# Latent attention: the key tiles' exponentials added on VectorE before one sum over partitions on TensorE

## The chip, the cores and the metric

The kernel runs on one core of one Trainium2 chip, in one launch. The metric is the device time of that core in microseconds (us). Five engines work in parallel, each in its own order: TensorE (PE, matmuls, with its weight loads PEld), VectorE (DVE), ScalarE (ACT), GpSimd (POOL) and SyncE (SP, DMA issues). They wait for one another through semaphores. SBUF is the on-chip memory, PSUM the memory into which PE writes.

## What is computed

The reference runs eight sub-layers one behind another (four attention or state-space layers, four feed-forward ones) over 16 sequences of 512 tokens with 128 features. The change is in the third, a causal attention with 16 heads whose keys and values come from a latent of 32 features:

```
q_blhd = jnp.einsum('bld,dhk->blhk', x_bld, Wq)
latent_bll = jnp.einsum('bld,dc->blc', x_bld, Wkv_down)
k_blhd = jnp.einsum('blc,chk->blhk', latent_bll, Wk_up)
v_blhd = jnp.einsum('blc,chk->blhk', latent_bll, Wv_up)
attn = jnp.einsum('bqhd,bkhd->bhqk', q_blhd, k_blhd) / jnp.sqrt(jnp.asarray(HD, dtype=x_bld.dtype))
attn = jax.nn.softmax(jnp.where(mask, attn, neg_inf), axis=-1)
y_blhd = jnp.einsum('bhqk,bkhd->bqhd', attn, v_blhd)
return jnp.einsum('bqhd,hdo->bqo', y_blhd, Wout)
```

The softmax needs, for every query and head, the sum over the keys of the exponentials. That sum is what the change computes in another way.

## The kernel before

The kernel has three loops, over sub-layers 1 to 4, 5 to 8 and the end. Each takes two sequences (`PAIR`) in a pass, so the first loop has eight passes, and each of them holds the latent attention once.

The 16 heads of the two sequences are worked in eight quartets of four heads (`QUARTETS`, c = 0 to 7). The 512 keys of a head lie in four tiles of 128, key tile m with the 512 - 128m queries that may see it: 512, 384, 256 and 128 columns, 1280 a head. A quartet has six steps (u = 0 to 5), two heads in each: steps 0 and 1 handle key tile 0, steps 2 and 3 key tile 1, steps 4 and 5 key tiles 2 and 3 together. In step (c, u) of `twin_attention`

- PE computes the transposed scores of quartet c (keys on partitions, `scores_t`, L1779, with the negated row maxima added by a bf16 matmul, L1790) and the plain scores of quartet c + 2 (queries on partitions, `scores`, L1761). Both go to one of three double PSUM banks, `twin`, handed round in turn: a matmul waits until the bank's last reader is done.
- DVE takes the row maxima of the plain scores (`maxima`, L792), two quartets ahead. A maximum is two instructions, the operation and a read of the accumulator.
- POOL splits a quartet's maxima into three bf16 parts (`split`, L615 to L625), PE turns them (`turn_max`, L1843), ACT copies them (`take_max_rows`, L1463).
- ACT takes the exponentials of the transposed scores into one of six buffers of `at_pt` in `arena` (`exponents`, L1435), and POOL sets the masked corner to zero (`mask`, L597 and L601).
- PE multiplies the exponentials with the latent values (`values`, into bank 6) and with ones (`sums`, into bank 7), both in `weigh` (L1802), in matmuls with 32 output rows, one for each of the four heads.
- ACT turns the sums into reciprocals (`invert`: logarithm L1454, exponential L1456), and DVE multiplies the values with them (`divide`, L806).

For the sums this means 16 matmuls a quartet over all 1280 columns of each head, with b = 0, 1, 2 for the steps' pairs. In the program each fp32 matmul is one instruction; in the trace it is two. The order of an engine's work is the order in which the functions are called at the end of each step; in between the engines wait on counts of semaphores. The last quartets (c = 6, 7) have no plain scores and no maxima beside them, since there is no quartet c + 2; the values and sums of quartet 7 end in a ninth round.

`ring` is an SBUF tensor of six rows of 512 that other layers use.

## Time and profile before

| | us |
|---|---|
| median of 3 runs | 6033.78 |
| lowest, highest | 5996.2, 6043.12 |
| span of the profiled execution | 6032.4 |
| PE busy in it | 4713.6 (78%) |
| DVE busy | 3697.0 (61%) |
| ACT busy | 1851.2 (31%) |
| POOL busy | 2161.3 (36%) |

The profiled execution is one execution of the program. Times inside it are counted from its first instruction. Busy time of an engine is the time covered by its instructions; matmuls overlap one another, so a group of them is priced by the distance between starts. In the timeline each row is a run of like instructions: start, length, engine, line, operation, output and inputs, shapes, and how many there are. A row of windows names its stretch and its length, the busy time (and count of instructions) of PE, PEld, DVE, ACT and POOL, the granted clock, the DMA share and GB/s. A bracket at the end of a timeline row is the idle time in front of it and who ended it. PEclk is the granted clock of PE, 1.00 for 2.4 GHz and 0.50 for 1.2 GHz.

### The profile page before, as it was taken

To read this page: it belongs to the slowest core of one execution; us is meant where nothing else is said; L and a number is where in the kernel's file an instruction comes from. 1 tells how busy PE (TensorE), PEld (TensorE's weight loads), DVE (VectorE), ACT (ScalarE), POOL (GpSimd) and SP (SyncE) were. 2 spreads that over 40 slices of the span, in tenths; PEclk is the share of its full clock that TensorE was granted. 3 is DMA by queue.
4 is the path that set the end of the run, shared out by engine and by line. 5 is a ranking of instruction groups with operands and counts; after the bars stand their busy time and mean duration, and the time that the engine had idled before them with its cause. 6 is when DMAs were issued, how large, how long until landed. Compare 5 with 4: busy or idle time off the path is not lost. (4 is left out here: it accounts for less than half of the span.)

```text
span 6032.4 us, 97232 instructions
## 1 busy us (share of the span) xinstructions
PE 4713.6 (78%) x37160; PEld 2735.5 (45%) x37160; DVE 3697.0 (61%) x11081; ACT 1851.2 (31%) x2829; POOL 2161.3 (36%) x2704
## 2 busy tenths in 40 slices
PE   5979797979797979595877868778687786877772
PEld 3444445444444444363443544535435444354442
DVE  3646464646464646364768567686686766857765
ACT  2333343334333334242323224132331322412320
POOL 1323232323232222444525236153361443614525
PEclk9989898989898989797888888888888888888886
DMA  4000000000000000372000000000000000000000
GB/s 146 6 18 6 18 6 18 6 18 6 18 6 18 6 18 6 112 232 74 4 15 13 8 20 4 15 14 6 18 6 12 18 5 17 8 9 20 3 15 5
DMA packets 141914, 146.71 MB, mean 24 GB/s; under 512 B 31256, under 2 KB 126042, under 8 KB 141042
## 3 DMA queue, kind: packets, MB, share of 16 engines
q1 hardware_dynamic: 114274, 93.48, 5.3%
q0 software_dynamic: 18432, 37.79, 2.2%
q10 hardware_dynamic: 8736, 8.91, 0.5%
q8 instruction: 326, 5.34, 0.4%
q14 instruction: 146, 1.20, 0.1%
HBM read 69.64 MB, written 62.59 MB: 22 GB/s over the span
## 5 line engine op out<-in xcount | busy, mean ns | idle before, releaser
L792 DVE CUSTOM_DVE_ANT_0 twin<-twin,w_mask_row 128x512 f32<-128x512 f32 (+3 forms) x2048 | 951.0, 521 | 329.7 <-PE twin L1761 328.3
L1761 PE MATMUL twin<-arena 32*128 32x128 f32 (+3 forms) x4096 | 799.4, 517 | 39.6 <-DMA arena<-hres 16.8
L1779 PE MATMUL twin<-arena 32*128 32x128 f32 (+3 forms) x4096 | 784.2, 499 | 35.3 <-DVE arena L792 33.9
L1707 PE MATMUL twin<-w_ident_b 128*128 128x512 bf16 x1536 | 454.9, 450 | 383.7 <-DVE mv L752 157.9
L1435 ACT ACTIVATE arena<-twin 128x768 f32<-128x768 f32 (+1 forms) x544 | 479.3, 881 | 691.6 <-PE twin L1790 387.5
L1779 PEld LDWEIGHTS twin<-arena 32*128 32x128 f32 x4096 | 342.8, 195 | 471.7 <-issue 283.3
L695 POOL TENSOR_SCALAR ve<-mv 128x4 f32<-128x4 f32 x128 | 27.7, 216 | 1467.8 <-DVE mv L752 1467.2
L321 POOL DMA_INDIRECT got<-sorted_y,back x288 | 281.1, 976 | 539.6 <-ACT ring L1641 289.0
L1707 PEld LDWEIGHTS twin<-w_ident_b 128*128 128x128 bf16 x1536 | 157.7, 112 | 651.5 <-DVE mv L752 180.6
L313 POOL DMA_INDIRECT sorted_x<-got,w_mo_first_slots x288 | 282.4, 981 | 467.5 <-DVE ring L866 302.2
L1761 PEld LDWEIGHTS twin<-arena 32*128 32x128 f32 x4096 | 353.6, 204 | 196.8 <-issue 109.2
L1802 PE MATMUL twin<-arena 128*32 128x128 f32 (+3 forms) x2944 | 305.8, 459 | 18.6 <-POOL arena L597 18.6
L792 DVE DVE_READ_ACCUMULATOR2_ANT arena<- 128x1 f32 x2048 | 292.4, 143 | 0.0
L597 POOL TENSOR_SCALAR_AFFINE_SELECT arena<-arena 128x256 f32<-128x256 f32 x352 | 143.0, 409 | 342.7 <-ACT arena L1435 342.5
L1435 ACT ACTIVATE ring<-twin 128x768 f32<-128x768 f32 (+1 forms) x224 | 194.0, 878 | 198.6 <-PE twin L1779 197.6
L701 POOL TENSOR_TENSOR rs<-ve,minus_half 128x4 f32<-128x4 f32 x208 | 223.6, 1075 | 17.3
L2180 PE MATMUL twin<-w_l3f_we,arena 128*128 128x128 f32 x1152 | 191.1, 320 | 47.7 <-DVE arena L1115 47.7
L651 POOL TENSOR_TENSOR w_mo_wgu<-w_mo_wgu,w_l_cs_feat 128x2048 f32<-128x2048 f32 x36 | 197.3, 5483 | 54.5 <-DVE w_mo_wgu L1364 27.7
L1802 PE MATMUL twin<-ring,arena 128*32 128x384 f32 (+3 forms) x1152 | 155.7, 497 | 64.1 <-POOL ring L597 57.5
L651 POOL TENSOR_TENSOR w_mo_wgu<-w_mo_wgu 128x2048 f32<-128x2048 f32 x36 | 200.3, 5568 | 13.5 <-DVE w_l_wo L1367 13.5
L2180 PEld LDWEIGHTS twin<-w_l3f_we,arena 128*128 128x128 f32 x1152 | 163.9, 221 | 88.9 <-DVE arena L1115 63.6
L1364 DVE TENSOR_REDUCE w_mo_wgu<-w_mo_wgu 128x128 f32<-128x1024 f32 x144 | 174.6, 1217 | 22.6 <-POOL w_mo_wgu L651 22.6
(440 smaller groups left out, 10008.1 us busy)
## 6 DMA issues: line engine op xcount, KB each, us to landing
sorted_y<-arena SPq DMA_DIRECT2D x96, 256.0 KB, 2.8
sorted_x<-zeros ACTq DMA_DIRECT2D x2, 4096.0 KB, 19.9
a<-sorted_x SPq DMA_DIRECT2D x64, 128.0 KB
b<-sorted_x SPq DMA_DIRECT2D x64, 128.0 KB, 2.5
hres<-sorted_x SPq DMA_DIRECT2D x64, 128.0 KB
sorted_x<-got,w_mo_first_slots POOLq DMA_INDIRECT x288
got<-sorted_y,back POOLq DMA_INDIRECT x288
x_out<-w_l_w SPq DMA_DIRECT2D x18, 256.0 KB, 2.3
```

Of the source, the lines that this page charges most:

```text
L313: pool.indirect_dma_start(sorted_x[r % GROUPS], bass.IndirectOffsetOnAxis(ap=slot_of[:, q, n:n + 1], axis=0), normed[q][:, r // GROUPS], N ...
L321: pool.indirect_dma_start(got[q][:, n], None, sorted_y, bass.IndirectOffsetOnAxis(ap=back[:, q, n:n + 1].bitcast(U32), axis=0)).then_inc(s ...
L651: pool.tensor_tensor(pr, left.broadcast_to(shape), right.broadcast_to(shape), ALU.mult).then_inc(sg["f_pool"], 1)
L701: pool.tensor_tensor(RS[q][:], VE[q][:], minus_half[:], ALU.pow).then_inc(sg["rstd_ready"], 1)
L792: last = dve.tensor_tensor_reduce(s[:, e, at:at + w], s[:, e, at:at + w], W["mask_row"][:, T - w:T], -1.0, 3e38, ALU.add, ALU.min, into)
L1364: i = dve.tensor_reduce(ht_sc[q][:, t, heads], ht_pr[m % 2].rearrange("p (h g d) -> p h g d", h=H, g=H)[:, heads], AX, ALU.add)
L1435: act.activation(at_pt[tag][n % len(at_pt[tag])][:, :, 0:w], twin[SLOT["scores_t", c, u] % 3][:, :, 0:w], ACT.Exp, scale=1.0 if tag == "l1 ...
L1707: pe.matmul(into, ident_b, ident_b.unsqueeze(1).broadcast_to([P, NT, P]), start=True, stop=True, skip_group_check=True)
L1761: last = pe.matmul(s[:, e, at:at + w], queries[r, P * i:P * (i + 1)], keys[r, 0:w], start=(at == 0), stop=True, skip_group_check=True)
L1779: last = pe.matmul(s[:, e, at:at + w], keys[r, P * m:P * (m + 1)], queries[r, P * m:T], start=(at == 0), stop=(tag == "l2"), skip_group_ch ...
L1802: last = pe.matmul(bank[into][rows_of(j), P * m:T], weights(m, j), at_pt[tag][n % len(at_pt[tag])][:, j % 2, at:at + w], start=(m == 0), s ...
L2180: i = pe.matmul(pb3(q, 3)[:, t], mo_fb[q][:, (e - 1) % 2, t * P:(t + 1) * P], weights[:, (e - 1) * P:e * P], start=(e == 1 and t == 0), st ...
```

## The change

DVE adds the exponentials of a head's key tiles where they share queries, into a new tile `at_sum` (two buffers in `ring`, 2 x 2 heads x 384 columns). Queries 0 to 127 see key tile 0 alone; their sum stays a matmul of 128 columns straight from the exponentials (`first_sums`). For queries 128 to 511 DVE adds tile 1 to tile 0 (`merge_first`, 768 elements for two heads), tile 2 to that (`merge_second`, 512) and tile 3 (`merge_third`, 256), and PE sums the result over the partitions once, with 384 columns a head (`merged_sums`). The sums of a quartet are 8 matmuls in place of 16. The exponentials now also wait until the additions and the first sums have read their buffer. `turn_max`, `values(c - 1, 2)`, `divide`, `invert` and `take_max_rows` move by one step. Layer 5's attention, which uses the same functions with the tag "l2", keeps its work and order.

```diff
+        at_sum = [ring[:, 3 * n:3 * (n + 1)].rearrange("p a t -> p (a t)").rearrange("p (h e k) -> p h e k", h=2, e=2)
+                  for n in range(2)]
...
+                            def merge_first(c, h):
+
+                                if not 0 <= c < QUARTETS:
+                                    return
+                                dve.wait_ge(sg["l1_masked"], STEPS_OF * c + 3 + h)
+                                if c >= 2:
+                                    dve.wait_ge(sg["l1_sums"], c - 1)
+                                dve.tensor_tensor(at_sum[c % 2][:, h], at_pt["l1"][h][:, :, P:T], at_pt["l1"][2 + h][:, :, 0:T - P],
+                                                  ALU.add).then_inc(sg["l1_merged"], 1)
+
+                            def merge_second(c, h):
...
+                                into = at_sum[c % 2][:, h, :, P:T - P]
+                                dve.wait_ge(sg["l1_masked"], STEPS_OF * c + 5 + h)
+                                dve.wait_ge(sg["l1_merged"], STEPS_OF * c + 2)
+                                dve.tensor_tensor(into, into, at_pt["l1"][4 + h][:, :, 0:2 * P], ALU.add
+                                                  ).then_inc(sg["l1_merged"], 1)
+
+                            def merge_third(c, h):
...
+                                into = at_sum[c % 2][:, h, :, 2 * P:T - P]
+                                dve.wait_ge(sg["l1_merged"], STEPS_OF * c + 3 + h)
+                                dve.tensor_tensor(into, into, at_pt["l1"][4 + h][:, :, 2 * P:3 * P], ALU.add
+                                                  ).then_inc(sg["l1_merged"], 1)
...
                                     beside(c, u)
-                                    if tag == "l2" and u == 1:
-                                        shift(c + 1)
-                                    if u == (2 if tag == "l1" else 5):
+                                    if tag == "l2":
+                                        if u == 1:
+                                            shift(c + 1)
+                                        elif u == 5:
+                                            divide(c - 1)
+                                    elif u < 2:
+                                        merge_second(c - 1, u)
+                                        if u == 1:
+                                            merge_third(c - 1, 0)
+                                            merge_third(c - 1, 1)
+                                    elif u == 3:
                                         divide(c - 1)
+                                    elif u >= 4:
+                                        merge_first(c, u - 4)
...
+                                    if tag == "l1":
+                                        act.wait_ge(sg["l1_merged"], STEPS_OF * (c - 1) + (1 + u % 2 if u < 4 else 5 + u % 2))
+                                        if u < 2:
+                                            act.wait_ge(sg["l1_first_sums"], c)
...
-                                    if tag == "l1" and u == 1:
+                                    if tag == "l1" and u == 2:
                                         invert(c - 1)
-                                    if tag == "l1" and u == 2:
+                                    if tag == "l1" and u == 3:
                                         take_max_rows(c + 1)
...
+                            def first_sums(c):
...
+                                for j in range(HG):
+                                    last = pe.matmul(bank[7][rows_of(j), 0:P], W["ones"][:, 0:LAT],
+                                                     at_pt["l1"][1 - j // 2][:, j % 2, 0:P], start=True, stop=True,
+                                                     skip_group_check=True)
+                                last.then_inc(sg["l1_first_sums"], 1)
+
+                            def merged_sums(c):
...
+                                pe.wait_ge(sg["l1_merged"], STEPS_OF * (c + 1))
+                                for j in range(HG):
+                                    last = pe.matmul(bank[7][rows_of(j), P:T], W["ones"][:, 0:LAT],
+                                                     at_sum[c % 2][:, 1 - j // 2, j % 2], start=False, stop=True,
+                                                     skip_group_check=True)
+                                last.then_inc(sg["l1_sums"], 1)
...
                                         elif u == 1:
-                                            sums(c - 1, 2)
+                                            values(c - 1, 2)
                                         elif u == 2:
+                                            merged_sums(c - 1)
+                                        elif u == 3:
                                             turn_max(c + 1)
-                                            values(c - 1, 2)
-                                        elif u == 3:
-                                            sums(c, 0)
                                         elif u == 4:
                                             values(c, 0)
                                         else:
-                                            sums(c, 1)
+                                            first_sums(c)
```

On PE, in the latent attention of a pass, the place is steps 0 to 3 of the second quartet (c = 1). `w_ones` marks the sums over partitions, `w_ident_b` the turned maxima, the other rows with 32 partitions the values. Before:

```order
L1802 MATMUL twin<-arena 32x384 x4
L1779 MATMUL twin<-arena 128x512 x2
L1790 MATMUL twin<-arena,w_ones_b 128x512 x2
L1761 MATMUL twin<-arena 128x512 x2
L1802 MATMUL twin<-arena,w_ones 32x256 x4
L1802 MATMUL twin<-arena,w_ones 32x128 x4
L1779 MATMUL twin<-arena 128x384 x2
L1790 MATMUL twin<-arena,w_ones_b 128x384 x2
L1761 MATMUL twin<-arena 128x384 x2
L1843 MATMUL twin<-w_ident_b,arena 128x128 x4
L1802 MATMUL twin<-arena 32x256 x4
L1802 MATMUL twin<-arena 32x128 x4
```

The same place in the changed kernel:

```order
L1847 MATMUL twin<-arena 32x384 x4
L1824 MATMUL twin<-arena 128x512 x2
L1835 MATMUL twin<-arena,w_ones_b 128x512 x2
L1806 MATMUL twin<-arena 128x512 x2
L1847 MATMUL twin<-arena 32x256 x4
L1847 MATMUL twin<-arena 32x128 x4
L1824 MATMUL twin<-arena 128x384 x2
L1835 MATMUL twin<-arena,w_ones_b 128x384 x2
L1806 MATMUL twin<-arena 128x384 x2
L1873 MATMUL twin<-ring,w_ones 32x384 x4
```

The values of key tiles 2 and 3 have moved one step forward, to where the sums of those tiles were, and the one sum of the added tile stands behind the scores of step 2; the turned maxima follow a step later.

On DVE the place is steps 5, 0 and 1 (`L794` are the maxima, each with its readout). In the changed kernel:

```order
L794 ISA twin,arena<-twin,w_mask_row 128x128
L794 ISA arena 128x1
L828 TENSOR_TENSOR ring<-arena 128x768
L794 ISA twin,arena<-twin,w_mask_row 128x512
L794 ISA arena 128x1
L794 ISA twin,arena<-twin,w_mask_row 128x512
L794 ISA arena 128x1
L838 TENSOR_TENSOR ring<-ring,arena 128x2x256
```

and then, behind the maxima of step 1:

```order
L794 ISA arena 128x1
L838 TENSOR_TENSOR ring<-ring,arena 128x2x256
L847 TENSOR_TENSOR ring<-ring,arena 128x2x128 x2
L794 ISA twin,arena<-twin,w_mask_row 128x384
```

Before, nothing stood between the maxima of these steps; the only other work was the divide behind those of step 2.

## Rows read from the trace of the kernel before

**Rows 1.** The page: busy time of each engine; POOL's mask (count, busy us, mean ns).

```profile
PE 4713.6 (78%) x37160; PEld 2735.5 (45%) x37160; DVE 3697.0 (61%) x11081; ACT 1851.2 (31%) x2829; POOL 2161.3 (36%) x2704
...
L597 POOL TENSOR_SCALAR_AFFINE_SELECT arena<-arena 128x256 f32<-128x256 f32 x352 | 143.0, 409 | 342.7 <-ACT arena L1435 342.5
```

**Rows 2.** Windows of one quartet with maxima beside it, and one without.

```profile
270.10:283.10 13.00, 13.00 (x152) 5.99 (x152) 8.51 (x33) 6.82 (x10) 6.02 (x14) 1.00 0.03 11
309.00:322.00 13.00, 13.00 (x123) 5.02 (x124) 1.38 (x2) 7.02 (x10) 5.20 (x9) 1.00 0.05 17
```

**Rows 3.** Timeline of PE in the first pass: start us, us, what.

```profile
266.91 0.86 PE L1802 MATMUL twin<-arena,w_ones 128*32 128x256 f32 x16
267.70 0.59 PE L1779 MATMUL twin<-arena 32*128 32x384 f32 x2
...
268.76 0.40 PE L1843 MATMUL twin<-w_ident_b,arena 128*128 128x128 bf16 x4
...
269.87 0.59 PE L1779 MATMUL twin<-arena 32*128 32x384 f32 x2
...
270.88 1.06 PE L1802 MATMUL twin<-arena,w_ones 128*32 128x512 f32 x8
271.88 0.81 PE L1779 MATMUL twin<-arena 32*128 32x256 f32 x6
...
273.28 1.06 PE L1802 MATMUL twin<-arena 128*32 128x512 f32 x8
...
275.67 0.85 PE L1802 MATMUL twin<-arena,w_ones 128*32 128x384 f32 x8
276.45 0.70 PE L1779 MATMUL twin<-arena 32*128 32x512 f32 x2
...
283.94 1.07 PE L1802 MATMUL twin<-arena,w_ones 128*32 128x512 f32 x8
```

**Rows 4.** Timeline of DVE there: maxima of step 5 and of step 0.

```profile
276.01 0.43 DVE L792 CUSTOM_DVE_ANT_0 twin<-twin,w_mask_row 128x256 f32<-128x256 f32 x1 [1.24 <-PE twin L1761]
...
277.23 0.14 DVE L792 DVE_READ_ACCUMULATOR2_ANT arena<- 128x1 f32 x1
277.90 0.70 DVE L792 CUSTOM_DVE_ANT_0 twin<-twin,w_mask_row 128x512 f32<-128x512 f32 x1 [0.52 <-PE twin L1761]
...
278.51 0.73 DVE L792 CUSTOM_DVE_ANT_0 twin<-twin,w_mask_row 128x512 f32<-128x512 f32 x1
279.16 0.14 DVE L792 DVE_READ_ACCUMULATOR2_ANT arena<- 128x1 f32 x1
```

**Rows 5.** Groups of DVE instructions, whole span: count, busy us, mean ns.

```profile
L890 DVE TENSOR_TENSOR arena<-arena,hres 128x512 f32<-128x512 f32 x32 | 22.2, 693 | 80.7 <-ACT hres L1508 80.7
...
L1334 DVE TENSOR_TENSOR arena<-arena 128x1024 f32<-128x1024 f32 x16 | 19.6, 1225 | 0.6
...
L1039 DVE TENSOR_TENSOR arena<-arena 128x256 f32<-128x256 f32 x16 | 6.8, 425 | 0.5
```

**Rows 6.** Timeline of ACT in the same quartet.

```profile
280.89 0.60 ACT L1454 ACTIVATE arena<-twin 128x512 f32<-128x512 f32 x1
...
282.06 0.79 ACT L1435 ACTIVATE arena<-twin 128x768 f32<-128x768 f32 x1
```

**Rows 7.** Timeline of POOL and DVE in layer 5's attention, two places.

```profile
2899.26 5.47 POOL L651 TENSOR_TENSOR w_mo_wgu<-w_mo_wgu,w_l_cs_feat 128x2048 f32<-128x2048 f32 x1
...
2904.21 2.32 DVE L1378 TENSOR_TENSOR w_mo_wgu<-w_mo_wgu 128x1024 f32<-128x1024 f32 x1
...
3290.39 1.71 DVE L1378 TENSOR_TENSOR w_mo_wgu<-w_mo_wgu 128x1024 f32<-128x1024 f32 x1
...
3290.96 1.41 POOL L597 TENSOR_SCALAR_AFFINE_SELECT ring<-ring 128x256 f32<-128x256 f32 x1
```

**Rows 8.** Timeline of PE and a window behind it, in layer 5's attention.

```profile
2944.32 0.85 PE L1802 MATMUL twin<-ring,arena 128*32 128x384 f32 x8 [1.71 <-POOL ring L597]
...
2946.20:2949.40 3.20, 3.20 (x27) 1.28 (x26) 0.00 (x0) 1.72 (x3) 3.20 (x1) 0.50 0.02 5
```

More of the change, by code:

```diff
@@ L817, in shift @@
                                                   ALU.add).then_inc(sg["l2_shifted"], 1)
+                            def merge_first(c, h):
[7 more added lines that the diff above has]
+                            def merge_second(c, h):
+                                if not 0 <= c < QUARTETS:
+                                    return
+                                into = at_sum[c % 2][:, h, :, P:T - P]
[4 more added lines that the diff above has]
+                            def merge_third(c, h):
+                                if not 0 <= c < QUARTETS:
+                                    return
+                                into = at_sum[c % 2][:, h, :, 2 * P:T - P]
+                                dve.wait_ge(sg["l1_merged"], STEPS_OF * c + 3 + h)
+                                dve.tensor_tensor(into, into, at_pt["l1"][4 + h][:, :, 2 * P:3 * P], ALU.add
+                                                  ).then_inc(sg["l1_merged"], 1)
                             for c in range(-2, QUARTETS + 1):
@@ L1806, in weigh @@
                                 return last
-                            def sums(c, b):
+                            def first_sums(c):
                                 if not 0 <= c < QUARTETS:
                                     return
-                                pe.wait_ge(sg["l1_masked"], STEPS_OF * c + 2 * b + 2)
-                                if b == 0:
-                                    pe.wait_ge(sg["l1_max_rows"], min(c + 2, QUARTETS))
-                                    if c >= 1:
-                                        pe.wait_ge(sg["l1_log"], c)
-                                last = weigh(c, b, 7, lambda m, j: W["ones"][:, 0:LAT])
-                                if b == 2:
-                                    last.then_inc(sg["l1_sums"], 1)
+                                pe.wait_ge(sg["l1_masked"], STEPS_OF * c + 2)
+                                pe.wait_ge(sg["l1_max_rows"], min(c + 2, QUARTETS))
+                                if c >= 1:
+                                    pe.wait_ge(sg["l1_log"], c)
+                                for j in range(HG):
[4 more added lines that the diff above has]
+                            def merged_sums(c):
+                                if not 0 <= c < QUARTETS:
+                                    return
+                                pe.wait_ge(sg["l1_merged"], STEPS_OF * (c + 1))
[4 more added lines that the diff above has]
+                                last.then_inc(sg["l1_sums"], 1)
                             def values(c, b):
```

## Prediction

> **What bounds the kernel now.** I read the page first: over the whole span PE is the busiest engine [rows 1], but that is an average over all layers, and the change lives in one of them, the latent attention (the third), which runs once in each of the eight passes of the first loop. So I took the windows of one such layer, one quartet of heads long. In a full quartet, where the score matmuls of two quartets ahead still run, PE is busy for the whole 13.00 us, at the full clock; DVE is busy 8.51 us, ACT 6.82, POOL 6.02; in the last quartets, where no scores are left, PE still fills the window and DVE has 1.38 us [rows 2]. PE is the bound there. The idle time of DVE in front of its maxima is put down to PE in the timeline too [rows 4]. From one quartet's first sums to the next one's it is 13.06 us (270.88 to 283.94). Of these, step 2 takes 2.17 (267.70 to 269.87) and steps 3 to 5 take 6.58 (269.87 to 276.45), so steps 0 and 1 take 4.31 [rows 3].
>
> **What PE loses.** Matmuls are pipelined, so I price a group by the distance from its start to the start of the next one. The sums cost 1.00 us for the four of 512 columns, 0.78 for 384 and 0.79 for 256 + 128 [rows 3]: 2.57 us a quartet. New are four of 384, again 0.78, and four of 128, which no row shows alone; between nothing and the 0.78 of the 384 I take 0.36 (the four of 128 inside the 0.79 group are at most 0.79 less some 0.5). So PE is relieved of 2.57 - 1.14 = 1.43 us a quartet and would need 11.64. If that were all: 1.43 x 8 quartets x 8 passes = 92 us, 1.5% of the span.
>
> **What DVE gains.** Six additions a quartet, all with both inputs and the output in SBUF: two of 768 elements, two of 512, two of 256. Such additions last 0.425 us at 256, 0.693 at 512, 1.225 at 1024 [rows 5]; 768 lies midway, 0.96. DVE overlaps the tail of one with the start of the next: a 0.70 us operation is followed after 0.61 us [rows 4], so in a row they cost 0.87, 0.60 and 0.34, 3.62 us together. DVE's 8.51 us become about 12.1, more than the 11.64 that PE needs. Already the totals say that at most some 1 us of 1.43 can come back in a full quartet.
>
> **Where the waits fall.** Work is in order on each engine, so I follow the chain. PE's new one-off sum stands in step 2 and waits for the last addition, which DVE does at the end of its step 1. DVE reaches it through its maxima of steps 4, 5, 0 and 1 with the additions behind them. Step 5's maxima start when PE's step 5 scores are done; from there DVE does not stop: 1.22 + 0.87, then 1.26 + 0.60, then 1.26 + 0.60 + 0.34 + 0.43 = 6.58 us (the maxima: 276.01 to 277.23, and 277.90 to 279.16 [rows 4]). Meanwhile PE does steps 0 and 1, reaches step 2 and has to wait there: it begins step 0 at the same moment, behind the new first sums (0.36 against the 0.34 until DVE starts, below), and has 4.31 + 1.06 us of work (267.70 to 268.76 for step 2's scores), so it stands still for about 1.3 us. Then the other half: the sum 0.78, step 3's scores 1.01 (269.87 to 270.88), the turned maxima 0.32 (what is left of step 2's 2.17 beside 1.06 for its scores and 0.79 for its values, which cost what the sums of that size do), step 4's scores 1.40 (271.88 to 273.28), the values 1.00 as the sums of 512 columns, step 5's scores 1.40 again, and 0.34 until DVE starts (275.67 to 276.01) [rows 3, 4]: 6.25 us. On this half ACT is late too: the logarithm and the reciprocal of the sums, 1.17 together, now come directly behind the sum and in front of step 3's exponentials, 0.79 [rows 6]. With a signal these end 2.1 us behind the sum, and PE wants to start the later half of step 4's scores, in the buffer that they read, some 0.5 us into the step, 1.8 us behind the sum; I put 0.25 on it. With 0.1 for a signal the loop is 6.58 + 6.25 + 0.25 + 0.1 = 13.2 us, against 13.06 now. **The gain of PE is turned into a wait for DVE; a full quartet stays where it was (+0.1).**
>
> The ends of a pass differ. The two sums of the first quartet (1.78 us) shrink to 0.36 and no merged sum falls in it yet: -1.2. The seventh quartet has no maxima beside it, DVE is free and PE keeps its 1.4 us. In the last one the additions, the sum, the logarithm, the exponential and the divide stand one behind another with nothing beside: +0.5. So a pass without anything else: 5 full quartets x 0.1 - 1.2 - 1.4 + 0.5 = -1.6 us, eight passes -13 us.
>
> **Two additions collide with POOL.** The trace has an addition with both inputs in SBUF that began while POOL worked on SBUF: it took 2.32 us where 1.22 is usual for 1024 elements [rows 5, 7], POOL's 5.47 us operation having begun 4.95 us before it; and where DVE's came first, POOL's 256-element mask took 1.41 us instead of 0.41 [rows 1, 7]. One waits for the other. In the chain above POOL's masks (0.41 us, twice that size in steps 4 and 5) and the small operations that split the maxima, directly behind step 5's, lie beside the additions of steps 0 and 1. Following exponentials to masks by the same durations, two of the six additions meet one: step 0's finds the split and the first mask in front of it, step 1's last one the mask of step 2, some 0.35 us each. Bounds: nothing, if the phases miss one another, and 0.41, a whole mask, for each of the four additions of those steps. I take 0.7 a full quartet, 1 us for the rest of the pass: 5 x 0.7 + 1 = +4.5 us a pass. POOL's own delays cost nothing while its 6.02 us of work, plus 3.6, fit into the quartet. The Trainium skill (SBUF — State Buffer, Who interferes with whom) says that a DVE instruction with two SBUF inputs and a GpSimd instruction that reads SBUF exclude each other for the whole instruction; by that rule the waits are there in every quartet, without it a pass ends at -1.6 us. The trace agrees with the rule.
>
> **The clock.** PE now has no gap in this layer, and the granted clock is 1.00, 2.4 GHz [rows 2]. It gets a gap of 1.3 to 2 us in each full quartet. In the attention of layer 5 PE was idle for 1.71 us and then busy again, and from 1.9 us later on the granted clock was 0.50, 1.2 GHz, over a stretch in which PE filled every moment [rows 8]. The work behind our gap (0.78 + 1.01 + 0.32 + 1.40 = 3.5 us) is on the loop, and at half the clock part of it counts: the stretch of [rows 8] was at least 3.2 us long, at half rate that is 1.6 us lost. Bounds: nothing, or 1.5 us in each of the five full quartets. I take one or two falls a pass, +2 us.
>
> **The sum.** -1.6 + 4.5 + 2 = +5 us a pass, +40 us over eight. The profiled execution has a span of 6032.4 us, the median of the runs is 6033.8, so nothing is to be corrected between them: 6073 us, 0.7% more than before. What this measurement can tell from no change is about 1% (60 us).
>
> **Rivals.**
> - *No collisions and no fall of the clock*: -13 us, 6021. For it: durations of POOL are short, the gap small. Against it: both rows shown. 0.22.
> - *PE's gain comes through*, the other side. It needs a DVE chain shorter than the loop: the additions would have to cost about 1.5 us less than my 3.62 on the full quartets, so 2.1 or less, and not collide. Then PE's 11.64 us bind and a pass wins 8 x 1.43 = 11.4 us at most, some 9 with its last quartet: 6032 - 72 = 5960. Against it: three rows of additions at one element in 1.04 ns. 0.06.
> - *The clock falls in nearly every full quartet*: 5 x 1.5 + 1 in place of 2 a pass, with the collisions: -1.6 + 4.5 + 8.5 = +11.4, 91 us: 6124. It decides from gaps of about 1.7 us on, which the collisions bring near. 0.27.
> - My forecast, small loss: 0.45.
>
> The change doing nothing at all can be left out: PE has 1.43 us less in each quartet for certain.
>
> **How the numbers follow.** The likeliest is 6073, with a range of its own of 6040 to 6105. The wide range takes the two neighbours in and leaves out the fast end: 6012 (-13 us, and a merge or two cheaper) to 6135. Faster by over 1% is the third case alone, 0.06. Within 1% are the first rival and about 0.85 of the forecast: 0.22 + 0.39 = 0.61, with a bit of the clock case 0.63. Slower by over 1%: 0.31.
>
> **What would show it.** In the windows of a full quartet after: length 13.2 to 14.5 us, PE busy some 11.7 and no longer the whole window, DVE above 11.5. In the timeline PE's gap in front of the 384-column sum on the added tile, released by DVE's 256-element addition, 1.3 to 2 us. DVE's additions: 0.96, 0.69, 0.43 alone, and up to 0.4 more where a mask runs. The granted clock in the layer: 1.00 or a little under. The seventh quartet shorter by 1.4 us. I am wrong if PE shows no gap there (then DVE's additions are cheaper or the maxima are done sooner than I follow), if ACT rather than DVE is named in front of the scores of step 4 with more than 0.3 us, or if layers other than this one change their length.

## The result and the profile after

| | before | after |
|---|---|---|
| median of the runs | 6028.69 (6 runs) | 5992.93 (6 runs) |
| lowest, highest | 5996.20, 6044.73 | 5984.18, 5993.93 |
| span of the profiled execution | 6032.4 | 5991.9 |
| PE busy | 4713.6 | 4611.8 |
| DVE busy | 3697.0 | 3921.0 |
| POOL busy | 2161.3 | 2256.5 |

The ratio is 0.9941, 95% interval [0.9918, 0.9965]: 36 us less, where 40 us more were forecast. It lies within the 1% called no change, but on the other side of it, with an interval that leaves out 1, and under the range's low end of 6012.

The page of the changed kernel, and its groups (busy us, mean ns, idle time in front and what ended it):

```profile
PE 4611.8 (77%) x36136; PEld 2726.6 (46%) x36136; DVE 3921.0 (65%) x11465; ACT 1848.7 (31%) x2829; POOL 2256.5 (38%) x2704
...
L828 DVE TENSOR_TENSOR ring<-arena 128x768 f32<-128x768 f32 x128 | 125.5, 981 | 4.8 <-POOL arena L599 4.8
L838 DVE TENSOR_TENSOR ring<-ring,arena 128x512 f32<-128x512 f32 x128 | 87.8, 691 | 24.3 <-POOL arena L603 22.6
L1873 PE MATMUL twin<-ring,w_ones 128*32 128x384 f32 x512 | 54.6, 498 | 38.6 <-DVE ring L847 38.6
L847 DVE TENSOR_TENSOR ring<-ring,arena 128x256 f32<-128x256 f32 x128 | 50.1, 431 | 0.0
```

The additions are priced as forecast (0.69 and 0.42 us; the 768-element one mostly 0.95). PE waits in front of the merged sum (L1873), and DVE's last addition ends that wait, 38.6 us in the whole span.

The windows of one full quartet, and of most of one without maxima beside it:

```profile
263.81:276.75 12.94, 12.08 (x133) 6.20 (x133) 11.50 (x40) 6.78 (x9) 7.40 (x14) 1.00 0.04 13
302.50:313.40 10.90, 10.90 (x110) 4.76 (x110) 4.78 (x7) 7.06 (x10) 7.36 (x9) 1.00 0.04 12
```

Against [rows 2]: PE no longer fills the full quartet, DVE has 11.50 in place of 8.51, POOL 7.40 in place of 6.02 without having more to do, and the clock is 1.00. The full quartet takes 12.94 us, where 13.06 was before and 13.2 forecast.

PE's timeline in that quartet (answering to [rows 3]), then DVE's (to [rows 4]), then POOL's:

```profile
263.81 0.85 PE L1873 MATMUL twin<-ring,w_ones 128*32 128x384 f32 x8 [0.86 <-DVE ring L847]
264.59 0.59 PE L1824 MATMUL twin<-arena 32*128 32x384 f32 x2
265.60 0.40 PE L1900 MATMUL twin<-w_ident_b,arena 128*128 128x128 bf16 x4
265.93 0.92 PE L1824 MATMUL twin<-arena 32*128 32x256 f32 x8
267.60 1.07 PE L1847 MATMUL twin<-arena 128*32 128x512 f32 x8
268.60 0.81 PE L1824 MATMUL twin<-arena 32*128 32x256 f32 x6
270.00 0.43 PE L1862 MATMUL twin<-arena,w_ones 128*32 128x128 f32 x8
270.35 0.70 PE L1824 MATMUL twin<-arena 32*128 32x512 f32 x2
...
270.12 0.43 DVE L794 CUSTOM_DVE_ANT_0 twin<-twin,w_mask_row 128x256 f32<-128x256 f32 x1 [0.22 <-PE twin L1806]
271.34 0.95 DVE L828 TENSOR_TENSOR ring<-arena 128x768 f32<-128x768 f32 x1
273.47 0.69 DVE L838 TENSOR_TENSOR ring<-ring,arena 128x512 f32<-128x512 f32 x1
275.33 0.69 DVE L838 TENSOR_TENSOR ring<-ring,arena 128x512 f32<-128x512 f32 x1
275.94 0.76 DVE L847 TENSOR_TENSOR ring<-ring,arena 128x256 f32<-128x256 f32 x2
...
270.61 0.63 POOL L603 TENSOR_SCALAR_AFFINE_SELECT arena<-arena 128x512 f32<-128x512 f32 x1 [0.90 <-ACT arena L1480]
271.55 0.86 POOL L617 CAST arena<-arena 128x16 bf16<-128x16 f32 x1 [0.31 <-DVE arena L794]
272.50 0.23 POOL L619 TENSOR_TENSOR arena<-arena 128x16 f32<-128x16 f32 x1
273.41 0.25 POOL L627 CAST arena<-arena 128x16 bf16<-128x16 f32 x1
273.55 0.87 POOL L599 TENSOR_SCALAR_AFFINE_SELECT arena<-arena 128x256 f32<-128x256 f32 x1
274.99 0.41 POOL L599 TENSOR_SCALAR_AFFINE_SELECT arena<-arena 128x256 f32<-128x256 f32 x1 [0.57 <-ACT arena L1480]
275.56 1.35 POOL L315 DMA_INDIRECT sorted_x<-got,w_mo_first_slots  x1 [0.16 <-issue]
```

From 270.12 DVE doesn't stop until the last addition is done, and PE starts the next merged sum at 276.75: 6.63 us. From 263.81 to 270.12 it is PE's half, 6.31. Step 4's scores take 1.67 (265.93 to 267.60) where 1.40 is their own length: the delay by ACT, as forecast. POOL's operations that began inside an addition are long: the cast at 271.55 took 0.86, where its like takes 0.25, the mask at 273.55 0.87, where 0.41 is usual. DVE's additions are not, though two of them begin while POOL is at work: the one at 273.47 inside the cast of 273.41, with 0.19 us of it left, the one at 275.33 inside the mask of 274.99, with 0.07 left. Both take 0.69.

The stretches between the starts of the divides on DVE (one in each quartet) split the layer, and they repeat in all passes of an execution to some hundredths of a us. In the table, "start" is from the first plain scores to the first divide; four full quartets follow, one that loses its maxima after the first steps ("fifth"), one without any ("sixth"), and the last. "First to last divide" reaches to the end of the last one (0.69 us more than the stretches' sum). "Rest" is from there to the next pass's first scores, the mean of seven. The e numbers are the experiments below.

| us | before | after | e5 before | e6 after | e1 after | e12 after | e4 | e3 | e7 | e11 |
|---|---|---|---|---|---|---|---|---|---|---|
| start (mean) | 39.3 | 39.6 | 39.4 | 39.7 | 39.6 | 39.7 | 39.8 | 38.7 | 38.9 | 38.9 |
| full quartet | 13.06 | 12.94 | 13.06 | 12.94 | 13.21 | 13.16 | 13.06 | 12.35 | 12.26 | 12.55 |
| fifth | 12.92 | 10.92 | 12.82 | 10.92 | 10.92 | 10.92 | 12.43 | 10.92 | 10.92 | 10.92 |
| sixth | 12.01 | 10.63 | 11.73 | 10.63 | 10.63 | 10.63 | 12.06 | 10.63 | 10.63 | 10.63 |
| last | 8.34 | 8.40 | 8.72 | 8.40 | 8.41 | 8.40 | 8.52 | 7.39 | 7.87 | 7.87 |
| first to last divide | 86.19 | 82.39 | 86.18 | 82.38 | 83.5 | 83.3 | 85.93 | 79.02 | 79.16 | 80.3 |
| rest (mean) | 176.3 | 173.5 | 175.4 | 177.7 | 178.8 | 180.3 | 177.1 | 178.1 | 173.7 | 176.6 |

The change moves the divide from step 2 to step 3, so these stretches do not begin at the same work before and after; only their total from the first scores to the last divide can be compared outright. For the ends of a pass PE's own marks are better, the starts of a quartet's first transposed scores (means of the eight passes, us; c counts the quartets from 0):

| | before | e5 before | after | e1 after | e4 | e3 |
|---|---|---|---|---|---|---|
| first plain scores to c = 0 | 19.5 | 19.7 | 18.8 | 18.9 | 19.5 | 18.9 |
| c = 0 | 13.09 | 13.09 | 11.37 | 11.37 | 13.09 | 11.37 |
| c = 1 | 13.06 | 13.06 | 12.93 | 12.94 | 13.06 | 12.01 |
| c = 2 to 5, each | 13.06 | 13.06 | 12.94 | 13.21 | 13.06 | 12.35 |
| c = 6 | 12.05 | 12.05 | 10.63 | 10.63 | 12.05 | 10.63 |
| c = 7 to the end of the last divide | 15.5 | 15.5 | 16.4 | 16.4 | 15.8 | 15.4 |

Of the 40.5 us between the two spans, 30.4 are the layer's (8 x 3.80), 2.0 are given back in "start", 19.8 lie in the seven rests, whose work the change doesn't touch, 3.4 ahead of the first layer; behind the last one 11.0 us are lost again. So about 28 us are the change's and the remainder had to be explained, or shown to be chance.

### The profile page after: what moved, and what is told of

Read it like the earlier page. It is cut to its first block and busy times, and to the rows that moved or that the text cites. A ratio compares the mean times of both kernels' runs of the same rounds, so it can differ in the third digit from the quotient of the medians.

```text
span 5991.9 us, 95904 instructions
## 1 busy us (share of the span) xinstructions
PE 4611.8 (77%) x36136; PEld 2726.6 (46%) x36136; DVE 3921.0 (65%) x11465; ACT 1848.7 (31%) x2829; POOL 2256.5 (38%) x2704
## 5 line engine op out<-in xcount | busy, mean ns | idle before, releaser
L794 DVE CUSTOM_DVE_ANT_0 twin<-twin,w_mask_row 128x512 f32<-128x512 f32 (+3 forms) x2048 | 949.5, 522 | 187.8 <-PE twin L1806 186.8
L315 POOL DMA_INDIRECT sorted_x<-got,w_mo_first_slots x288 | 309.0, 1073 | 454.1 <-DVE ring L907 284.9
L794 DVE DVE_READ_ACCUMULATOR2_ANT arena<- 128x1 f32 x2048 | 294.2, 144 | 0.0
L599 POOL TENSOR_SCALAR_AFFINE_SELECT arena<-arena 128x256 f32<-128x256 f32 x352 | 176.2, 503 | 284.3 <-ACT arena L1480 282.6
```

Of the source, the lines that this page charges most:

```text
L315: pool.indirect_dma_start(sorted_x[r % GROUPS], bass.IndirectOffsetOnAxis(ap=slot_of[:, q, n:n + 1], axis=0), normed[q][:, r // GROUPS], N ...
L599: pool.affine_select(p, p, [[0, 2], [1, P]], ALU.is_ge, 0.0, base=0, channel_multiplier=-1).then_inc(sg[tag + "_masked"], 1)
L794: last = dve.tensor_tensor_reduce(s[:, e, at:at + w], s[:, e, at:at + w], W["mask_row"][:, T - w:T], -1.0, 3e38, ALU.add, ALU.min, into)
```

## Experiments

Each group of four ran on one chip beside the kernel before, e1 to e4 on one, e5 to e8 and e9 to e12 on two others. A ratio is to the kernel before of the same group.

**e1, the changed kernel again.**

> The changed kernel once more, unaltered. In its first trace the latent attention from its first to its last divide takes 82.39 us in every pass (before: 86.19), 30 us over eight passes; the rest of the 40 us by which the spans differ lies outside the layer. Theory A (the layer alone is changed by the edit): the layer is 82.39 us again, the rest of a pass differs by some us in either direction, and the time is 0.4 to 0.6% below the kernel before. Theory B (the change also shortens what follows in a pass): the stretches outside the layer repeat their lengths of the first trace to within 1 us.

6039.78 us, ratio 0.9999 [0.9988, 1.001]. Neither theory holds whole. The layer did not come back at 82.39 but at 83.5 us: the full quartets took 13.21, the others the same as before to 0.01. And the rest took 178.8 us in place of 173.5. Two things vary from execution to execution: the full quartets and the rest.

**e5, the kernel before again, and e6, e12, the changed one.**

> The kernel before once more, unaltered, with a trace. e1 gave the changed kernel the same time as before (ratio 0.9999) although its latent attention was shorter by 2.7 us a pass than in the first trace of before (83.5 against 86.19). Theory A (the layer's gain is real, and the rest of a pass, where the granted clock falls, takes it back or not by its phase): the layer takes 86.2 us in every pass here too, full quartets 13.06, and the stretch from the last divide of a pass to the next pass's scores is shorter than the changed kernel's 178.8 us by 1 to 3 us. Theory B (the engines' own speed differs between the executions): the layer of before is shorter here too, about 85 us or less.

> The changed kernel a third time, to see how its full quartets fall: 12.94 us in its first trace, 13.21 in e1, in all passes of an execution. Theory A (two ways in which PE and ACT can lock in, decided by small phases): 12.94 or 13.21 again, nothing between, the same in most passes. Theory B (a spread that has nothing to do with the order): other values, differing from pass to pass. Time between 0.994 and 1.000 of the kernel before.

> The changed kernel beside e11 on one chip. Its layer takes 82.4 us (or 83.5, as in e1), 3 to 4 us a pass more than e11's. Theory A: ratio to before 0.994 to 1.000, and 25 to 35 us above e11. Theory B (it was luck on that chip that e7 was faster): within 10 us of e11.

e5: 6032.95, ratio 1.0013 [0.9993, 1.0033]. e6: 5984.09, 0.9947 [0.9923, 0.9972]. e12: 6036.24, 0.9986 [0.9971, 1.0]. Theory A in all three, with two sizes off: the rest of e5 is 3.4 us shorter than e1's, not 1 to 3, and e12 lies 42 us above e11, not 25 to 35. The layer of before is 86.18 again, that of the changed kernel 82.38 and 83.3: the layer's gain is in every trace, 2.7 to 3.8 us a pass. The rest is another matter. Inside the one execution of e5 it takes 172.0 to 178.0 us. Two windows of it, behind the first and the second pass's layer:

```profile
326.90:499.60 172.70, 130.33 (x1386) 90.75 (x1386) 98.73 (x303) 46.35 (x71) 31.38 (x42) 0.89 0.05 14
625.00:802.60 177.60, 136.94 (x1386) 93.27 (x1386) 98.31 (x302) 46.35 (x71) 31.38 (x42) 0.85 0.04 14
```

The same 1386 matmuls, nearly the same time on DVE, ACT and POOL, 4.9 us more at a granted clock of 0.85 in place of 0.89. This stretch has idle times of PE and low clocks in any kernel; how many it meets varies by pass. Summed over the seven rests of an execution it comes to 1214 to 1262 us in the six traces of the two kernels. e6's trace has 178.2 us in six of seven rests, and its span, 6029.5, is at the top of that kernel's runs, whose median is 47 us lower than the profiled run. So the 19.8 us that the first pair of traces showed there are no effect of the change that I could show. The opposite isn't shown either. In e1's group the layer's 20 us (0.33%) ought to be seen, the interval [0.9988, 1.001] leaves them out, and this over 12 runs and 23 of before; in e12's group [0.9971, 1.0] is just short of it too. There the changed kernel's granted clock over the whole span is also lower than that of before (medians 0.871 against 0.875, 0.8705 against 0.873), and its traced rests are long (178.8 and 180.3). Some 10 to 20 us came back outside the layer on these two chips, and whether the change has a part in it stays open.

The full quartets come at two lengths, not at one or at any: 12.94 (after, e6) and 13.16 to 13.21 (e12, e1). ACT's exponential of step 5 in e1 and in e6:

```profile
273.56 0.81 ACT L1480 ACTIVATE arena<-twin 128x768 f32<-128x768 f32 x1 [2.21 <-PE twin L1835]
```

```profile
270.62 0.81 ACT L1480 ACTIVATE arena<-twin 128x768 f32<-128x768 f32 x1 [1.84 <-PE twin L1835]
```

It waits for the same matmuls, which PE started at the same place of the quartet in both, and starts 0.36 us later in e1. From there all follows later: its bank, the next plain scores, their maxima. In e3, e9, e11 and e12 it comes late too (0.31 to 0.37 us, in the full quartets), in the other traces with the clock at 1.00 not. That the late signal makes the longer quartet is read from these traces: no run moves it by itself. DVE has the like in step 5 of the kernel before: in [rows 3, 4] the maxima start 0.34 us behind the sums' start (275.67 to 276.01), and in e5 0.12:

```profile
272.91 0.85 PE L1802 MATMUL twin<-arena,w_ones 128*32 128x384 f32 x8
...
273.03 0.43 DVE L792 CUSTOM_DVE_ANT_0 twin<-twin,w_mask_row 128x256 f32<-128x256 f32 x1 [1.03 <-PE twin L1761]
```

Both have a full quartet of 13.06: where PE is the bound, it costs nothing. What delays such a signal in one execution and not in another stays open.

**e4, DVE's additions alone, e3, PE's part alone.** e4 is the kernel before with

```diff
+                                    if tag == "l1":
+                                        if u < 2:
+                                            merge_second(c - 1, u)
+                                            if u == 1:
+                                                merge_third(c - 1, 0)
+                                                merge_third(c - 1, 1)
+                                        elif u >= 4:
+                                            merge_first(c, u - 4)
```

> DVE's part alone: PE's sums and the whole order stay as in the kernel before, and DVE makes the six additions of each quartet, which nobody reads. Theory A (DVE has room for 3.62 us beside PE's 13.0 and wins against POOL when both want SBUF): a full quartet stays at 13.06 to 13.3 us, the layer at 86.2 to 87.5, the time at 6029 to 6040; POOL's masks and its row transfers get longer. Theory B (the additions wait for POOL, as predicted, 0.7 us a full quartet, and PE waits behind them for its banks): the layer takes 90 us or more, the time 6060 or more.

6050.09, ratio 1.0015 [1.0001, 1.0028]. A full quartet is 13.06 as before:

```profile
270.50:283.50 13.00, 13.00 (x152) 6.04 (x148) 11.45 (x40) 6.87 (x9) 8.24 (x13) 1.00 0.03 11
```

PE has no gap; 11.45 us of DVE fit beside it, and no addition takes more than 0.96, 0.72 and 0.44 us. Theory A holds for the layer (85.93), though the time is 10 us above its range. POOL has 8.24 us in place of 6.02 [rows 2]: it is the one that pays for sharing SBUF.

e3 is the changed kernel without the additions (the exponentials of steps 4 and 5 wait for the sum in their place), with

```diff
-                                                     at_sum[c % 2][:, 1 - j // 2, j % 2], start=False, stop=True,
+                                                     at_pt["l1"][5 - j // 2][:, j % 2, 0:T - P], start=False, stop=True,
```

> PE's part of the change alone: the same matmuls as in the changed kernel (128 + 384 columns a head), but the 384 columns come straight from the exponentials of key tiles 2 and 3, and DVE adds nothing, so the sums leave out key tile 1 and most of tile 0. Theory A (the DVE chain ate part of PE's gain): PE is the bound, a full quartet takes 11.7 to 12.1 us, the layer about 77.5, the time about 5955. Theory B (PE's gain was never there, since the exponentials or the banks set the pace): a full quartet takes 12.9 and the time is 5993.

5986.97, ratio 0.9909 [0.9897, 0.9922]. PE fills the quartet (window 262.30 to 274.60: busy 12.30 of 12.30); its 12.35 us are 0.25 above A's span, in an execution where ACT's signal of step 5 came late; the first full quartet of each pass, ahead of which it wasn't late, takes 12.01. The time is 32 us above A's and 6 below B's, the mechanism is A's: DVE's chain costs the changed kernel 0.86 us of the quartet in e1, on the same chip.

**e10, POOL's masks twice.**

```diff
+                                if tag == "l1":
+                                    pool.affine_select(p, p, [[0, 2], [1, P]], ALU.is_ge, 0.0, base=0,
+                                                   channel_multiplier=-1).then_inc(sg["l1_twice"], 1)
+                                    pool.wait_ge(sg["l1_twice"], n + 1)
```

> POOL makes each mask of the latent attention twice, one behind the other (0.41 us more in steps 0 to 3, 0.64 in steps 4 and 5, 2.9 us a quartet), so it is on SBUF more often beside DVE's additions. Theory A (where both want SBUF, POOL is the one that waits, as in the first trace of the changed kernel): DVE's additions keep 0.95, 0.69 and 0.42 us in full quartets, those stay at 12.94 to 13.2 us, the time changes by less than 10 us. Theory B (an addition that finds POOL at work waits for it, as predicted): additions of the full quartets get longer by up to 0.4 us each, full quartets take 13.4 us or more, the time is longer by 15 to 50 us.

6109.72, ratio 1.0109 [1.008, 1.0137], where e12 on the same chip has 0.9986: 73 us more, above theory B's 50. Theory B by mechanism. A full quartet takes 13.51 us, 0.57 more than 12.94 (no signal came late in it). DVE's and POOL's timelines there:

```profile
276.27 1.16 DVE L836 TENSOR_TENSOR ring<-arena 128x768 f32<-128x768 f32 x1
278.67 1.09 DVE L836 TENSOR_TENSOR ring<-arena 128x768 f32<-128x768 f32 x1
282.81 0.90 DVE L846 TENSOR_TENSOR ring<-ring,arena 128x512 f32<-128x512 f32 x1
283.63 0.97 DVE L855 TENSOR_TENSOR ring<-ring,arena 128x256 f32<-128x256 f32 x2
...
275.98 0.64 POOL L611 TENSOR_SCALAR_AFFINE_SELECT arena<-arena 128x512 f32<-128x512 f32 x1
276.77 1.50 POOL L315 DMA_INDIRECT sorted_x<-got,w_mo_first_slots  x1 [0.16 <-issue]
278.29 0.65 POOL L608 TENSOR_SCALAR_AFFINE_SELECT arena<-arena 128x512 f32<-128x512 f32 x1
282.76 0.41 POOL L600 TENSOR_SCALAR_AFFINE_SELECT arena<-arena 128x256 f32<-128x256 f32 x1
283.23 0.74 POOL L603 TENSOR_SCALAR_AFFINE_SELECT arena<-arena 128x256 f32<-128x256 f32 x1
```

Each of the four began 0.05 to 0.40 us after a mask, with 0.27 to 0.36 us of it left, and took 0.14 to 0.21 longer than alone. The first of them (276.27) costs nothing: in the changed kernel DVE stands idle for 0.22 us behind it. The other three lie between step 5's maxima and the merged sum: 0.14 + 0.21 + 0.21 = 0.56 of the 0.57 us. It is the order of starts that decides who waits, and what is left of the first one that decides how long. A mask with 0.56 us left cost the addition 0.42 (once a pass, in the last quartet of the changed kernel, 1.37 us), with 0.20 left 0.06 (e1, 1.01 us), with 0.07 left nothing. [rows 7] has the like: the addition at 3290.39 took 1.71 us, 0.49 more than usual, with 0.63 us left of an operation that POOL had begun at 3285.54. The Trainium skill (SBUF — State Buffer, Who interferes with whom) says that issue order and not the operation decides who blocks; these two traces agree.

Of the 73 us this is 5 x 0.57 x 8 = 23. The rest is not: the longer masks also delay the last quartets (sixth stretch 11.72, last 11.46), and in every layer of e10 the clock fell for 3 to 15 us. PE's first gap of a pass was 1.69 us there, and the clock fell behind it in four of the eight passes; the gaps of the following full quartets, 1.42 to 1.53 us nearly everywhere, were in no pass followed by a fall in these quartets.

**e2, the merged sum a step later; e8 and e9, a longer chain.** e2:

```diff
-                                        elif u == 2:
-                                            merged_sums(c - 1)
                                         elif u == 3:
-                                            turn_max(c + 1)
+                                            merged_sums(c - 1)
                                         elif u == 4:
+                                            turn_max(c + 1)
                                             values(c, 0)
```

> The merged sum moves from step 2 to step 3 of the next quartet, and with it the inversion, the turned maxima and the divide, a step each. Theory A (a full quartet is a loop of DVE from step 5 to the last addition, 6.63 us, and of PE from the merged sum to step 5's scores, 6.31 us; PE waits 0.86 us in it): behind step 3's scores the sum no longer waits, and a full quartet falls from 12.94 to PE's own 12.1 us or DVE's 12.05; the layer from 82.39 to about 78.6 us, the time by 30 us to 5963. Theory B (ACT's logarithm in front of the exponentials takes the place of the wait): the quartet stays at 12.9 and the time at 5993.

6233.53, ratio 1.0318 [1.0305, 1.0331]: neither theory. The wait before the merged sum is gone, but I had moved the divide behind step 4's maxima, and the values of step 4 wait for it, 1.78 us:

```profile
241.56 1.07 PE L1847 MATMUL twin<-arena 128*32 128x512 f32 x8 [1.78 <-DVE a L808]
255.80 1.07 PE L1847 MATMUL twin<-arena 128*32 128x512 f32 x8 [1.78 <-DVE b L808]
```

Full quartets in a row, by windows:

```profile
240.73:254.97 14.24, 12.46 (x132) 6.34 (x132) 11.44 (x42) 6.89 (x9) 7.42 (x14) 1.00 0.03 10
254.97:272.19 17.22, 15.44 (x132) 6.96 (x132) 11.69 (x42) 6.89 (x9) 6.98 (x14) 0.80 0.03 9
```

The first costs 1.3 us more by the wait alone, the next another 3.0 by the clock. So the clock rival of the prediction exists, though the changed kernel doesn't meet it. How near it is was asked of DVE's chain: e8 has two idle operations of 512 elements in front of the last additions, e9 one:

```diff
+                                into = at_sum[c % 2][:, :, :, 0:P]
+                                dve.wait_ge(sg["l1_extra"], c)
+                                dve.tensor_tensor(into, into, into, ALU.max).then_inc(sg["l1_extra"], 1)
```

> Two more DVE operations of 512 elements (0.60 us each, the maximum of a piece of the added tile with itself, which leaves it as it is) stand in front of the last additions of each quartet; PE's wait in front of the merged sum grows from 0.86 to about 2.1 us. Theory A (the loop is DVE's chain plus PE's half, and the clock stays): a full quartet takes 14.15 to 14.4 us, the granted clock in it is 1.00, the layer is longer by 5 us, the time by 45 us. Theory B (a gap of PE of 1.7 us and more is followed by a fall of the clock, as in e2, where full quartets of 14.24 became 17.2): quartets of 16 to 17.5 us with the clock at 0.50 in part of them, the time longer by 120 us or more. Quartets with DVE idle don't change by more than 0.3 us in either.

> One more DVE operation of 512 elements (0.60 us) in front of the last additions of each quartet, in place of the two of e8. PE's gap before the merged sum becomes about 1.5 us. Theory A (the loop is a sum of DVE's chain and PE's half): a full quartet takes 13.54 us (12.94 + 0.60) or 13.8 (13.21 + 0.60), the layer 84.8 to 86, 20 us more than the changed kernel in all, and the granted clock in the layer stays at 1.00. Theory B (the clock falls already at such gaps): the layer takes over 95 us with the clock at 0.50 in a part of it, the time is longer by 80 us or more.

e8: 6236.45, ratio 1.0357 [1.0314, 1.0401], full quartets 14.5 to 20.6 from divide to divide, PE's gap in a full quartet 2.39. e9: 6225.45, ratio 1.0304 [1.0261, 1.0346]. e9's full quartets and the one behind them:

```profile
238.57:252.67 14.10, 12.39 (x138) 6.04 (x136) 12.60 (x41) 6.78 (x10) 7.37 (x14) 1.00 0.03 10
...
280.90:295.48 14.58, 12.87 (x130) 5.93 (x128) 12.60 (x41) 7.06 (x10) 7.54 (x14) 0.93 0.03 10
295.48:315.04 19.56, 19.56 (x110) 7.69 (x108) 7.68 (x26) 5.95 (x8) 7.73 (x13) 0.50 0.03 8
```

Theory B in both. e9 without a fall has quartets of 14.10, 0.9 above e12's 13.16 on the same chip: 0.60 for the operation and some 0.3 because one of the two last additions now met POOL behind its row transfer and took 0.75 us. The gap was 1.71 us, that of [rows 8]. In this pass the clock held for three quartets and then fell, in other passes of e9 it fell in the first or the third, and a quartet in which PE has work for every moment took 19.56 us for 10.92. The changed kernel's 0.86 (0.78 in e1) never did that, in 4 traces of 8 layers each.

**e7 and e11, a version from this.** The chain wants to be shorter, and PE stands idle in front of the merged sum. So tile 3 is not added by DVE; PE sums it there with four matmuls of 128 columns, except in quartets 5 and 6, where DVE has nothing else:

```diff
+                                if c not in (5, 6):
+                                    pe.wait_ge(sg["l1_masked"], STEPS_OF * (c + 1))
+                                    for j in range(HG):
+                                        pe.matmul(bank[7][rows_of(j), 3 * P:T], W["ones"][:, 0:LAT],
+                                                  at_pt["l1"][5 - j // 2][:, j % 2, 2 * P:3 * P], start=False, stop=False,
+                                                  skip_group_check=True)
+                                pe.wait_ge(sg["l1_merged"], 4 * (c + 1))
```

> Tile 3 isn't added by DVE but summed by PE with four matmuls of 128 columns straight in front of the merged sum, where PE stood waiting for 0.86 us, except in quartets 5 and 6, where DVE is idle. DVE's chain is shorter by two additions of 256 elements (0.34 us each). Theory A (in the changed kernel DVE's chain ends last in a full quartet): the quartet falls from 12.94 or 13.2 to 12.4 to 12.6 us (PE is busy 12.08 and gets 0.36 more), the layer to about 80.5, 15 to 25 us less in all than the changed kernel. Theory B (PE's work or ACT's exponentials set the pace): 0.36 us longer in each full quartet, 13.3 to 13.6, 14 us more in all.

> The kernel of e7 once more (tile 3 summed by PE in the gap, full quartets 12.26 us, layer 79.16). Theory A (the gain lies in the layer): layer 79.2 us again, the ratio to before at 0.985 to 0.993. Theory B (the clock's phases made it): the ratio comes to 0.995 or more.

e7: 5954.92, ratio 0.9894 [0.9865, 0.9923]; e11: 5994.67, 0.9931 [0.9909, 0.9952], a layer of 80.3 and not 79.2, and so the edge of A's range. On either chip it beats both kernels: 29 and 42 us under the changed one (e6, e12). The full quartet is 12.26 (12.55 in e11, where ACT's signal came late), and PE has no gap:

```profile
260.40:272.66 12.26, 12.26 (x146) 6.37 (x144) 10.82 (x40) 6.78 (x10) 7.39 (x14) 1.00 0.04 13
...
269.44 0.43 PE L1876 MATMUL twin<-arena,w_ones 128*32 128x128 f32 x8
269.70 0.85 PE L1883 MATMUL twin<-ring,w_ones 128*32 128x384 f32 x8
```

The four matmuls cost 0.26 in place of a wait of 0.86, and theory A's 12.4 to 12.6 was even too high.

## Why the prediction was wrong

- **The bound and the mechanism: right.** PE was the bound; with the additions a full quartet is DVE's chain and PE's half, one behind the other, and most of PE's 1.43 us turns into a wait of 0.86 released by DVE's 256-element addition. The sum forecast +40 us; its wrong terms are these.
- **DVE's half: right.** 6.58 + 0.1 forecast, 6.63 measured; the additions' prices too. ACT's delay 0.25 forecast, 0.27 measured; PE's first sums 0.36 and 0.35.
- **PE's half: mis-sized by one term.** The "0.34 until DVE starts" was read from one execution of a PE-bound kernel, in which nothing hung on it. It is 0.12 in the changed kernel, and in e5 in the kernel before. That is 0.22 of the 0.26 us between 13.2 and 12.94. PE's gap was 0.86 and not 1.3: 0.22 by the same term, 0.17 because PE's way from step 0 to the gap took 5.54 us (270.35 to 275.89) and not 5.37. In e1 and e12 another signal is late by 0.31 to 0.37, and the quartet comes to 13.16 to 13.21: that the forecast's length is met there is luck.
- **The ends of a pass: right in kind, short in size.** The seventh quartet (c = 6) gave the forecast 1.4 us (12.05 to 10.63). The first (c = 0) gave 1.7 where 1.2 was put, the last cost 0.9 where 0.5 was put. Left out altogether was the stretch ahead of the first quartet, 0.7 us shorter; e3 has it without the additions and e4, the additions alone, hasn't, so it comes with the new order on PE, by which wait stays open. From its first scores to its last divide a pass is 3.5 us shorter (86.19 - 82.39 less 0.3) where -1.6 was forecast: 5 x 0.22 = 1.1 of the difference are the full quartets (-0.12 each for +0.1), 0.5 and 0.7 the first one and what is ahead of it, less 0.4 at the end.
- **The collisions, +4.5 us a pass, 36 of the forecast 40 us: the step that failed most.** They exist, and the one that comes second waits (e10). The two additions that I named do begin while POOL is at work, in every full quartet, but I gave each a wait of 0.35 us and they wait for nothing, because POOL's operation is at its end, with 0.2 and 0.07 us left; the phases had been followed over several durations and were off by a few tenths. In e1 the mask of step 5 had 0.20 left and the addition took 1.01 in place of 0.95, that of step 1 0.72 in place of 0.69. Elsewhere in the quartet it is POOL that comes second, and it has 5 us to spare and pays.
- **The clock, +2 us a pass: nothing.** The granted clock stays at 1.00 through the layer. The mechanism and its price were real, and harder than put: e9's gap of 1.71 us costs 3% of the kernel, above the 6124 of that rival. But the falls in full quartets came behind gaps of 1.69 us and more (e2, e8, e9, e10), and ours is half of that, since the gap came out at 0.86 in place of the 1.3 to 2 that I gave it.
- **The size in all.** The layer gives 3.5 us a pass at best and 2.5 in e1 and e12 (83.4 against 86.18, less 0.3), 28 or 20 us: 0.3 to 0.5%. The four comparisons gave 0.59, 0.01, 0.53 and 0.14%: the layer's gain and what happens outside the layer. The first result, 36 us, was on the large side.

## What to carry to other kernels

When work is moved from the bounding engine to another, follow the other's chain to its end and leave it a margin: here two short additions given back to PE, in the place where it stood waiting, won more than the change itself. A latency read while it hides behind another bound is one sample of something that may have two values; put both in the range. And where two engines wait for one another, as DVE's additions and POOL's operations do here, the cost falls on the one that comes second and depends on what is left of the first, so settle who that is and how much is left, to a tenth of a us, or put both outcomes in the range; then ask whether the one that waits has time to spare.

## What the runs showed of the hardware

- An addition with two SBUF inputs also lengthens POOL's issue of an indirect DMA that starts inside it: 1.35 us at 275.56 in place of 0.97 at 268.74 in the changed kernel, 1.50 in e10.
- An addition with two SBUF inputs that starts inside a mask of POOL is longer by about 0.14 us less than what is left of the mask: +0.42 with 0.56 left, +0.21 with 0.35 left, +0.14 with 0.27 left (after, e10).
- A wait of PE of 0.86 us in every quartet leaves the clock at 1.00, and so did the waits of 1.42 to 1.53 us in e10's full quartets. One of 1.71 us, repeated every 14.1 us, or of 1.78, every 14.2, is followed by a fall, in some passes at once, in others after one to three quartets; the clock then stays at 0.50 even where PE is busy throughout (19.56 us of it in e9).
- A signal from PE to ACT or DVE behind the same matmuls came at one of two times, 0.22 us (DVE) or 0.31 to 0.37 us (ACT) apart, the same in the full quartets of an execution.
